# Decoder layer: one output weight block of four split a step later on GpSimd, and the last two steps reordered

## The reference

```python
x = _layernorm(x + _L0_attn_ref(x, ...))
x = _layernorm(x + _L0_xattn_ref(x, ctx_4096, ...))
x = _layernorm(x + _L0_ffn_ref(x, ...))

# cross attention: 32 query heads of 128 in 8 groups, one key and value head a group
q = query @ Wq + bq;  k_, v_ = split(kv @ Wkv + bkv)
attn = softmax(einsum('blkgd,bmkd->bkglm', q, k) * scale)
o = einsum('bkglm,bmkd->blkgd', attn, v);  return o @ Wo + bo

# last part
z = x @ W.T + b;  u = x @ A (8 experts x 16);  m = einsum(u, B, p_scores)
gamma = minimum(0.5 * norm(z) / (norm(m) + 1e-6), 1);  return z + gamma * m
```

## Time and profile before

| | |
|---|---|
| median of 3 runs | 2814.56 us (2813.96 to 2815.39) |
| profiled execution, its own time | 2814.78 us |
| its span, first to last instruction | 2813.0 us |
| mean granted TensorE clock | 0.991 |
| second stage, steps 4 to 63, from the first score product to the last projection | 1713.3 to 2736.5 us |
| last stage | 2736.5 to 2813.0 us |

### The profile page before, as it was taken

The page is one execution under the profiler, slowest core; times in us unless marked ns, Lnnn a source line. Parts: engine busy times, 40 slices in busy tenths (PEclk is TensorE's granted clock), DMA queues, the critical chain, the costliest instruction groups (busy, mean ns, idle before and its releaser), DMA issues.

```text
span 2813.0 us, 63696 instructions
## 1 busy us (share of the span) xinstructions
PE 2729.2 (97%) x26368; PEld 2377.6 (85%) x26368; DVE 1956.3 (70%) x3893; ACT 1463.7 (52%) x3079; POOL 1596.7 (57%) x1363
## 2 busy tenths in 40 slices
PE   7999999999999999999999999999999999999987
PEld 6888889889888888888888878788888887878766
DVE  5666666676676676666666767766677777676777
ACT  5565665666565665665656544433334344333335
POOL 6887887888777666766666742232225322232225
PEclk9999999999999999999999999999999999999999
DMA  5223313323424231232222221111112111111011
GB/s 174 81 84 105 96 59 105 107 64 90 110 86 148 81 86 50 79 87 72 71 82 81 66 83 42 34 42 42 45 34 64 42 42 42 34 42 34 31 31 60
DMA packets 91481, 197.68 MB, mean 70 GB/s; under 512 B 20664, under 2 KB 21304, under 8 KB 89144
## 3 DMA queue, kind: packets, MB, share of 16 engines
q1 hardware_dynamic: 71480, 154.80, 19.1%
q10 hardware_dynamic: 17664, 34.61, 3.6%
q0 software_dynamic: 2048, 4.20, 0.5%
HBM read 176.78 MB, written 16.78 MB: 69 GB/s over the span
## 4 chain that ended last, share of the span: by engine, by line
PE 89%; DVE 5%; issue 2%; POOL 2%; ACT 1%; DMA 0%; ACTq 0%; DVEq 0%
PE big L1823 30%; PE bank L1823 30%; PE big L1895 14%; PE bank L1915 12%; PE big L1915 2%; POOL ptl L778 1%; DVE nmx L1383 0%; DVE P L1389 0%; DVE z L1514 0%; DVE stat L1751 0%; DVE xol L1479 0%; PE big L1816 0%; DVE P L1653 0%; POOL oTl L783 0%; POOL gathered L753 0%
## 5 line engine op out<-in xcount | busy, mean ns | idle before, releaser
L778 POOL TENSOR_TENSOR ptl<-P,pth 128x576 fp32r<-128x576 f32 x512 | 725.3, 1436 | 238.4 <-ACT pth L954 237.6
L945 ACT ACTIVATE P<-big,nmx 128x576 f32<-128x576 f32 x512 | 378.6, 740 | 404.2 <-DVE nmx L1383 399.1
L1389 DVE STREAM_TRANSPOSE P<-P 128x576 f32<-128x576 f32 x512 | 387.7, 767 | 149.8 <-ACT P L945 147.6
L1915 PE MATMUL bank<-pth,v 32*128 32x256 f32 x4608 | 423.6, 280 | 4.6 <-DVE xacc L1411 1.4
L1915 PE MATMUL big<-pth,v 32*128 32x256 f32 x4608 | 423.8, 281 | 0.0
L1915 PEld LDWEIGHTS bank<-pth,v 32*128 32x128 f32 x4608 | 382.5, 186 | 17.1 <-issue 14.4
L854 POOL TENSOR_TENSOR P<-P,sm 128x512 f32<-128x512 f32 x64 | 67.3, 1051 | 578.9 <-DVE sm L1676 578.9
L1383 DVE TENSOR_REDUCE nmx<-big 128x1 f32<-128x576 f32 x512 | 372.6, 745 | 7.2 <-PE big L1895 5.2
L954 ACT ACTIVATE pth<-P 128x576 fp32r<-128x576 f32 x512 | 347.6, 682 | 51.1 <-DVE P L1389 48.4
L1915 PEld LDWEIGHTS big<-pth,v 32*128 32x128 f32 x4608 | 362.9, 186 | 0.0
L1915 PE MATMUL bank<-ptl,v 32*128 32x256 f32 x2304 | 350.1, 278 | 0.0
(11 more groups left out here) (289 smaller groups left out, 7867.5 us busy)
## 6 DMA issues: line engine op xcount, KB each, us to landing
rall<-kept_r ACTq DMA_DIRECT2D x64, 512.0 KB
raw<-in_wo SPq DMA_DIRECT2D x64, 256.0 KB
raw<-in_xWq SPq DMA_DIRECT2D x64, 256.0 KB
raw<-in_xWo SPq DMA_DIRECT2D x64, 256.0 KB
raw<-in_wq SPq DMA_DIRECT2D x62, 256.0 KB
v<-kept_v SPq DMA_DIRECT2D x24, 448.0 KB
v<-kept_v SPq DMA_DIRECT2D x68, 128.0 KB, 3.3
raw<-in_xWkv SPq DMA_DIRECT2D x32, 256.0 KB
```

The costliest lines, as they stand in the source:

```text
L778: pool.tensor_tensor(third_columns(ptl, i), blocks_of(i), f(third_columns(pth, i)), ALU.subtract).then_inc(p_low(i), 1)
L945: act.activation(P[:, i % PSLOTS, :].rearrange("p (k n) -> p k n", k=2), ps_s[i % 2][:, :, 0:HALF], ACT.Exp, bias=nmx[:, i % 8:i % 8 + 1], ...
L1389: dve.transpose(P[:, i % PSLOTS, :], P[:, i % PSLOTS, :]).then_inc(p_turned(i), 1)
L1915: m = pe.matmul(ps_o[a][:, 0:256], v[r, s, l, :], p[r, lo:hi + 1:hi - lo, block_of(b), :, :], start=first, stop=final)
```

## The change

Of the four blocks `wo2` of a group, the fourth is split in step 4g + 1: on ACT behind `out2_hi` and ahead of the step's first query and its exponential, on POOL ahead of its multiplication. POOL makes three of the four low parts, DVE one. The order of the loads stays. In step 62 the tiles 4 and 5 and `low_rank(0)` go ahead of the projections, the three weight blocks are split ahead of ACT's exponential and POOL's multiplication, and `out2_lo` goes ahead of DVE's maximum. In step 63 tiles 6 and 7 and both linear products go ahead of the projections, and `out2_lo` goes behind the sum. `low_rank(1)` moves from tile 3 of the last stage to the place between `values2(63)` and `project2(63)`, in a bank that no longer depends on `low_rank(0)`.

```diff
 def blocks_at(g, s):
     if s == 0:
-        return [("wo2", 4 * g + j) for j in range(4)]
+        return [("wo2", 4 * g + j) for j in range(3)]
...
+def late_block(g, s):
+    return [("wo2", 4 * g + 3)] if s == 1 else []
...
-        line += [("ctx", t) for t in tiles_at(n // 4, n % 4)] + blocks_at(n // 4, n % 4)
+        g, s = n // 4, n % 4
+        line += late_block(g, s) + [("ctx", t) for t in tiles_at(g, s)] + blocks_at(g, s)
...
+LAST_BANKS = [(("w", STEPS - 1, 0), 3), (("w", STEPS - 1, 1), 1)]
...
-            return (kind == "wo2" and n % 2 == 1) or ...
+            return (kind == "wo2" and n % 4 == 1) or ...
 # POOL, step n
+                for a in late_block(g, s):
+                    weight2(*a)
                 for tt in tiles_at(g, s):
                     weight2("ctx", tt)
+                if n == STEPS - 2:
+                    for a in work:
+                        weight2(*a)
                 gate.wait_ge(rec_done, (2, n))
...
-                for a in work:
-                    weight2(*a)
+                if n != STEPS - 2:
+                    for a in work:
+                        weight2(*a)
 # ACT, step n
                     out2_hi(n - 1)
                     next_value_hi(n - 1)
+                for a in late_block(g, s):
+                    weight2(*a)
                 for m, j in units(n)[:1]:
                     query2_hi(m, j)
-                if last:
+                if n >= STEPS - 2:
                     for tt in early_x3(n):
                         tile_high("x3", tt)
+                if n == STEPS - 2:
+                    for a in work:
+                        weight2(*a)
                 gate.wait_ge(max_done, (2, "sub", n))
                 act.activation(flat(P2[:, :, :]), ..., ACT.Exp, scale=SCALE)
+                if n == STEPS - 2:
+                    low_rank_hi(0)
...
-                if not last:
+                if n < STEPS - 2:
                     for tt in early_x3(n):
                         tile_high("x3", tt)
-                if n == STEPS - 2:
-                    low_rank_hi(0)
-                for a in work[:2]:
-                    weight2(*a)
+                    for a in work:
+                        weight2(*a)
                 if g + 1 < GG:
                     key2_hi(g + 1, s)
-                for a in work[2:]:
-                    weight2(*a)
 # DVE, step n
                     dve.transpose(P2[own, :, :], ps_sc[own, :, cols])
+                if n == STEPS - 2:
+                    out2_lo(n - 1)
...
-                if n >= 1:
+                if 1 <= n < STEPS - 2:
                     out2_lo(n - 1)
                     next_value_lo(n - 1)
-                if last:
+                if n >= STEPS - 2:
                     for tt in early_x3(n):
                         tile_low("x3", tt)
                 gate.wait_ge(exp_done, (2, n))
                 dve.tensor_reduce(sm2[:, :], pv, AX.X, ALU.add)
+                if last:
+                    out2_lo(n - 1)
...
+                if n == STEPS - 2:
+                    low_rank_lo(0)
                 if last:
                     z_out(0)
                 gate.wait_ge(p_norm, (2, n))
...
+                if last:
+                    z_out(1)
                 add_out2(n - 1, 0)
                 add_out2(n - 1, 1)
...
+            out2_lo(STEPS - 1)
             statistics(pairs2(GG - 1, 2), 2)
-            z_out(1)
-            out2_lo(STEPS - 1)
 # TensorE, step n
-                if last:
-                    for tt in early_x3(n):
-                        turn_acc("x3", tt)
-                    linear(0)
-                project2(n - 1, 0)
-                project2(n - 1, 1)
-                if not last:
+                if n >= STEPS - 2:
                     for tt in early_x3(n):
                         turn_acc("x3", tt)
                 if n == STEPS - 2:
                     low_rank(0)
                 if last:
+                    linear(0)
                     linear(1)
+                project2(n - 1, 0)
+                project2(n - 1, 1)
+                if n < STEPS - 2:
+                    for tt in early_x3(n):
+                        turn_acc("x3", tt)
...
             values2(STEPS - 1)
+            low_rank(1)
             project2(STEPS - 1, 0)
             project2(STEPS - 1, 1)
...
-                if tt % 4 == 3 and tt // 4 + 1 < 4:
+                if tt % 4 == 3 and 2 <= tt // 4 + 1 < 4:
                     low_rank(tt // 4 + 1)
```

More of the change, by code:

```diff
@@ L496, in low_on_dve @@
         def low_on_dve(kind, n):
-            return (kind == "wo2" and n % 2 == 1) or (kind == "x" and (n < 6 or n >= HT and n % 2 == 0)) or (kind, n) in (("wq", 0), ("wq", 1), ("wk", 0), ("wv", 0))
+            return (kind == "wo2" and n % 4 == 1) or (kind == "x" and (n < 6 or n >= HT and n % 2 == 0)) or (kind, n) in (("wq", 0), ("wq", 1), ("wk", 0), ("wv", 0))
         def wait_split(gate, kind, n):
@@ L1277, in bank_order @@
             at = {("u", q): ps_u for q in range(1, 4)}
-            for key, b in FIRST_BANKS:
+            for key, b in FIRST_BANKS + LAST_BANKS:
                 at[key] = q_banks[b]
@@ L1292, in bank_order @@
                     put(("q", m, j))
-                if n == STEPS - 1:
-                    for tt in early_x3(n):
-                        put(("x3", tt))
-                if n >= 1:
-                    put(("w", n - 1, 0))
-                    put(("w", n - 1, 1))
-                if n < STEPS - 1:
+                if n >= STEPS - 2:
                     for tt in early_x3(n):
@@ L1303, in bank_order @@
                     put(("u", 0))
+                if n >= 1:
+                    put(("w", n - 1, 0))
+                    put(("w", n - 1, 1))
+                if n < STEPS - 2:
+                    for tt in early_x3(n):
+                        put(("x3", tt))
                 if n == 0:
@@ L1310, in bank_order @@
                         put(("v", g + 1, s))
-            put(("w", STEPS - 1, 0))
-            put(("w", STEPS - 1, 1))
             for tt in range(HT, NT):
@@ L1696, in vector_program @@
                     statistics(pairs2(g, n - STEPS + 2), 2)
-                if n == STEPS - 2:
-                    low_rank_lo(0)
-                for a in work[:2]:
+                for a in work:
                     weight2(*a)
@@ L2009, in tensor_program @@
                          4: (kv_lo, ("k", 0, 0)), 5: (kv_lo, ("k", 0, 1)), 6: o_free[2], 7: o_free[3]})
-            first_bank = dict(FIRST_BANKS)
+            own_bank = dict(FIRST_BANKS + LAST_BANKS)
             ring = [1]
@@ L2019, in q_bank @@
             def q_bank(key, released):
-                if key in first_bank:
-                    b = first_bank[key]
+                if key in own_bank:
+                    b = own_bank[key]
                 else:
@@ L2143, in low_rank @@
                 else:
-                    gate.wait_ge(ff_lo, ("u", q - 1))
                     if q == 1:
                         bank_free(2)
+                    else:
+                        gate.wait_ge(ff_lo, ("u", q - 1))
                     ps = ps_u
```

## The result

The changed kernel takes **2780.01 us** (median of 4 runs, 2776.66 to 2783.67), the kernel before 2814.97 in the runs beside it (4 runs, 2813.96 to 2815.44). The ratio is **0.9877**, 95% interval 0.9859 to 0.9894: faster by 1.2%, and 1.0 us from the predicted 2781. The profiled execution is the longest of the four: 2783.67, with a span of 2781.8 us.

The account below looks back on a forecast made before the run. TensorE, busy 97% of the span, was taken as the bound, so only gaps and low clock could give time. 17.1 + 5.9 + 1.0 + 9.9 = 33.9 from 2814.78 gives 2780.9, median 2781; range 2776 to 2786 (60%).

Parts of the forecast that it names:

- Late steps: Seven steps n = 4g + 1 of even groups, 19.2 us over together, keep 0.3 each: 17.1 us gained.
- Step 1: Second stage, step 1 (20.80 us): the late block lands after DVE's subtraction, nothing collides, all 5.9 us go.
- Step 29: A tile's turn there waits on the heads' low part because of the late block: 1.0 us gained.
- Step 61: Projection starts 2.3 us earlier and no 1.6 us low clock follows, so step 62 starts 3.9 us earlier.
- Step 62: Softmax chain becomes the bound, with 2.2 us for POOL's splits meeting maximum and subtraction; `values2(62)` starts at 2701.8.
- To the last stage: From `values2(62)`: 22.2 us of products, 1.0 of waits, and 1.6 given back for one low clock stretch.
- The last stage: Loses `low_rank(1)`, 2.8 us of TensorE, but runs on the ACT and DVE exchange: stays 76.5 us.
- 1 (the lock costs more): Rival, 12%: POOL's late split stops two DVE instructions in turn, or ACT reaches it later: 2791 us.
- 2 (nothing collides, 2775): Rival, 14%: no collisions and the clock stays up; 2.1, 1.6 and 2.2 us come back: 2775 us.
- 3 (the clock falls more often): Rival, 7%: four more low clock stretches at 1.6 us: 2787 us.
- 4 (late loads): Rival, 4%: ACT's late split waits for its load ahead of the exponential, 16 times; slower, 2825 us.
- 5: Rival, 3%: no effect; the projection waits as long for the heads' high part or the fourth block: 2814 us.

Follow-up runs that it names:

- e3: Kernel before with only the fourth block's low part given to POOL, at its old place in step 4g; 2783.1 us, ratio 0.988.
- e9: Changed kernel with the late block's low part on DVE again, behind `out2_lo` in step 4g + 1; 2776.05 us, ratio 0.9864.
- e5: Changed kernel with POOL's late split held back until DVE has subtracted the maximum; 2778.6 us, ratio 0.9876.
- e4: Changed kernel with POOL's late split held until the subtraction, and step 62's weight splits behind ACT's exponential and around POOL's low part; 2772.46 us, ratio 0.9845.
- e7: Changed kernel with `low_rank(1)` back at tile 3 of the last stage; 2778.92 us, ratio 0.9877.
- e2: Kernel before with only the new order of steps 62 and 63 and the moved `low_rank(1)`; 2809.94 us, ratio 0.9979.
- e8: e4 with the norms of steps 9 and 41 moved to steps 13 and 45 of odd groups; 2769.92 us, ratio 0.984.

## Why the prediction was right, step by step

**Late steps, 17.1: right.** The seven steps behind step 1 with 19.2 us over 14.88 now take 15.17 each, 0.29 over, so 17.2 are gained, for the reason given: DVE turns its scores at once, and one row of swaps (1.79) is the price. The forecast had DVE end the heads' low part 8.1 to 8.3 us into step 33; it ends at 8.07. Behind this stand e3 and e9 (it is the place ahead of the scores alone) and e5 (take the collision away and the 0.29 goes). **Step 1, 5.9: right**, 20.80 to 14.87.

**Step 29, 1.0: undersized.** It was sized by its one booked wait, and the length of the step went from 20.13 to 18.66, 1.5 us. Some 0.16 of the difference is the model: the wait counts from the shown end of a product (0.39 long) and not from the turn of the next (0.23 on). The other 0.3 is the eight products that the wait held up, which take 1.31 us behind it and 1.04 in the changed kernel:

```profile
2141.22 1.31 PE L1816 MATMUL big<-ident,xaccb 128*128 128x128 f32 x8 [1.02 <-DVE xol L1479]
```

```profile
2132.61 1.04 PE L1833 MATMUL big<-ident,xaccb 128*128 128x128 f32 x8
```

The step's length was the number to take.

**Step 61, 3.9: right.** 20.08 to 16.16. Of its gap of 1.55 us, 1.06 is one DVE instruction of the maximum beside POOL (1.24 for 0.17): in e4 the step takes 15.10.

**Step 62: the total right, the cause half wrong.** From the start of step 62 to `values2(62)` the prediction has 16.5 us (2685.3 to 2701.8); the trace has 16.54 (2665.01 to 2681.55). But the prediction put 2.2 us of it on the maximum and subtraction beside POOL's splits, with ACT's third split landing about when the exponential could start. The loads came later: maximum and subtraction paid nothing, the exponential waited 1.8 and a swap of the sum 1.1, in all 2.9 for 2.2. The rest of the chain was shorter by as much. That the sizes agree is partly luck; the failing step is the landing time of the three blocks, which the rows of before didn't hold for the new order.

**To the last stage: 1.0 too long, and no term right.** The prediction has 22.2 + 1.0 + 1.6 = 24.8 us from `values2(62)` on; the trace 23.81. The products alone take some 22.9 (e4 and e5 without their wait). The 1.0 was a wait of `linear(0)` (0.6) and of the last projections on the heads' low part (0.4): neither came in this trace, though the first shows in e5 (0.2) and e4 (0.6), where the clock stayed up. The low clock stretch came, behind the largest gap (3.44) and not from "four gaps close together", and cost about 1.0.

**The last stage, unchanged: right** (76.44 against 76.47), and e7 shows it from the other side. One thing in it was not foreseen: `low_rank_out(4)` now comes 2.0 us ahead of the low part that it needs, since the tile before no longer has `low_rank(1)` to do. It costs nothing in this trace; where a low clock stretch follows it, the stage takes 0.7 us more (last section).

**The sum:** 17.2 + 5.9 + 1.5 + 10.8 (67.35 to 56.51 from step 61 to the last stage) = 35.4 of the 35.5 measured, against 33.9 predicted. The sum is 1.5 short: 0.5 in step 29 and 0.9 behind `values2(62)`. The profiled run itself is only 31.1 us shorter than before's, since its first stage took back 4.3, and the medians differ by 35.0. That the median comes within 1.0 us of the forecast is therefore in part luck; the windows are what bears the sum out.

**The signs.** The late steps, step 1, the swap of 1.2 us on DVE, the 11 us and the last stage came as listed. "No wait of TensorE over 1 us on `xol`" did not: steps 10 and 42 keep theirs of 1.6 each, which stood in the trace of before. The wait on `xpl` was to be about 2 us and was 3.44: the prediction had a wait for tile 4's bank take 1.1 us of it, and that wait doesn't show.

**The rivals.** 1 (the lock costs more) is out: one stall a step, and e5's 1.1 on the subtraction shows that one is what an instruction pays. 2 (nothing collides, 2775) is out: the swaps took 1.79; e4, in which nothing collides in the late steps and in steps 61 to 63, takes 2772.46. 3 (the clock falls more often) is out: from step 1 to the end of the products the trace has one stretch, and not five. 4 (late loads) is out, but the case for it came up: ACT had the late block without a wait in the seven late steps, and waited for its load 1.9 us in step 1 and 1.6 in step 61, ahead of the exponential. Neither held the step up: step 1 takes 14.87, and in step 61 the exponential still waits 1.4 us for DVE behind the split. 5 is out: the steps are shorter.

## What to carry to other kernels

Where an engine writes out its own order, look for a wait on a DMA that stands ahead of work on the critical chain: moving that one instruction behind the chain (or to another engine) gave nine tenths of the gain here (31.8 us of 35.0), and the rest of the change little. Cost each step of such a change by the step's window and not by its booked waits. When work is moved to GpSimd, place it beside VectorE instructions that read PSUM, and hold it back with a wait if need be: one wait more in each of 16 steps made seven of them 0.3 us shorter and one 1.06.

## What the runs showed of the hardware that was not expected

**Like gaps, two clocks.** In the last stage `low_rank_out(4)` waits 1.95 to 1.99 us in the six kernels with the new end and the moved product. In e2, e4 and e8 the granted clock falls to 1.2 GHz for 3.4 us about there, and their last stage takes 77.1 to 77.2 us; in the changed kernel, e5 and e9 it stays at 2.4, and the stage takes 76.4 to 76.5 us. Ahead of `values2(62)` gaps of 2.56 (e9) and 2.77 us (e5) brought no such stretch, while 2.73 (e2), 3.29 (e7) and 3.44 did. From step 1 on, the shortest gap with one behind it is 1.80 us (step 17 of e2), and no gap up to 1.6 us had one in any trace. That is no safe bound: near 1600 us, in the first stage, all ten traces have two gaps close together, of 1.26 and some 1.67 us, and in three of them (the changed kernel, e3, e8) the clock falls there. What else decides stays open.

**The first stage is the noise.** Code that is the same word for word ends between 1646.7 and 1654.5 us in nine traces of kernels other than the one before. The trace of the changed kernel is the latest, with four low clock stretches in the first 100 us (20.5 us together) and 6.8 us at 1603; e4 is the earliest, with 6.8 us of them in all. The stretches are not the whole of it: e5 and e9 have 6.8 us each and end 2.1 us apart. So a difference of 4 us between two single executions of this kernel can lie in code that is the same; compare windows of the changed steps instead.
